# Attention with mixture of experts: the turned sums move to the second pass's ring, and the scaling of the outputs to GpSimd

## The chip, the cores and the metric

The kernel runs on one core of a Trainium2 chip. The metric is the device time of one execution in microseconds (us), as the median of several runs. The engines are TensorE (PE, with its weight loads as PEld), VectorE (DVE), ScalarE (ACT), GpSimd (POOL) and SyncE (SP), which only issues DMAs here. SBUF is the working memory, PSUM the memory that TensorE writes and that VectorE and ScalarE read.

## The reference

The input `x` has shape (8, 1024, 256). With `xn` the layer norm of `x`, the result is

```
x + attention(xn) + ffn(xn)
kqv   = xn @ W_kqv.T                      # 16 heads of 16
score = q @ k / 16 + slope[h] * (n - s)   # per head, key position n, query position s
attention = softmax(score) @ v
ffn = sum over the two best of 8 experts of w * swiglu_e(xn), plus a shared swiglu
```

The softmax needs, for each query of each head, the maximum of its 1024 scores; both sums over keys (of `exp * v` and of `exp`) come from one matrix product, since `v` carries a column of ones.

## The kernel before

Three stages follow each other: `front` (layer norm, projections, shared expert, routing), `experts` (the routed experts, whose results go to a scratch tensor `yr`) and `attend` (attention, and the combination of everything into the output). The change is in `attend` alone.

`attend` works through 32 groups, each of four heads (`GH`) of one batch (8 batches, 4 groups each). A group has 64 units (`UNITS`), in two halves of 32 (`HALF`); a half is 512 queries (`HQ`) against 8 blocks of 128 keys (`NK`) for four heads. In a document like this one a pair is two successive units, and pair k of a group begins with unit 2k.

In each unit `n` TensorE issues one `score` (128 keys by 512 queries, into `p2`, a ring of three PSUM banks) and one half of a maximum unit of the next group (`max_half`, into `p1`, a ring of two tiles, each of two banks). In every odd unit it adds four `products` (probabilities by values, into `p_o`), for a block of keys whose exponentials are done: in units 4k+1 and 4k+3 for units 4k-4 to 4k-1. ScalarE takes the exponential of each `p2` bank into `probs`. VectorE reduces each `p1` tile of 128 by 1024 to its maxima (`max_unit`), one in each pair; eight of them make a chunk, which `join` (two inputs in SBUF) combines to eight columns of `neg`. So one group's first pass (maxima) runs beside the previous group's second pass.

The maxima must become a row of `q_op`. For each of the four chunks of a group `turn_max` transposes `neg` on TensorE into a `p2` bank, ScalarE copies the 8 rows to `m_row`, and SP sends them by two DMAs. The turns are placed by hand: the own group's chunk 3 after unit 5 (`OWN_TURN`), the next group's chunks 0, 1 and 2 after units 21, 37 and 53 (`TURN_AT`).

The output of a half leaves in this way. After unit 3 of the following half ScalarE copies `p_o` to `o_sb` (`output_copy`). After unit 13 (`OUT_TURN`) TensorE transposes it in four pieces into an entry of the first pass's ring `p1` (`turn_output`). VectorE, in its place among the maxima, inverts the sums (`reciprocal`, L1216) and multiplies (L1220) into `att`, a ring of two batches; it adds one to `s1_read` only then, and the ring has two places, so the next maximum unit on TensorE needs the reduction before the output to have ended.

GpSimd waits until four groups of a batch are in `att`, and then, in loops with registers, combines its eight blocks one after another (`combine`): loads of `base` and two gathers from `yr`, the addition of `att`, two scalings and two additions, a store. The last batch is combined by VectorE from terms gathered ahead (`last_terms`, `final`).

Every engine runs its instructions in program order. The groups are written out for all engines but GpSimd.

Of the kernel before, what the change touches and what calls it, by code (L numbers as in the profile page):

```python
# [16 lines left out]
F32 = mybir.dt.float32  # L17
# [5 lines left out]
ds = bass.ds  # L23
# [927 lines left out]
def attend(nc, keep, scratch, out):  # L951
    with ExitStack() as ctx:
# [9 lines left out]
        neg = [sb(f"neg{i}", [P, 8], F32R) for i in range(2)]  # L962
        m_row = [sb(f"m_row{i}", [8, P], F32R) for i in range(4)]
        o_sb = [sb(f"o_sb{i}", [P, HQ]) for i in range(2)]
        rec = sb("rec", [P, 4, GH])
# [6 lines left out]
        col_i = [sb(f"col_i{i}", [P, 2], I32) for i in range(2)]  # L972
        col_w = [sb(f"col_w{i}", [P, 2]) for i in range(2)]
# [11 lines left out]
                 "ex_ok w_ready dve_w pool_c o_st0 o_st1 c_ok base_in0 base_in1 yg_in0 yg_in1 fin_base fin_y "  # L985
# [4 lines left out]
        m_in = [sem(f"t_m_in{c}") for c in range(4)]  # L990
# [9 lines left out]
        OUT_ENTRY = (OUT_TURN + 1) // 2  # L1000
        SIDE = HQ // 2
        R1 = MAX_UNITS + 2
        R2 = UNITS + CHUNKS
        K_LOAD = 14

        def ring1(g, first):
            return MAX_UNITS if first else g * R1 + (MAX_UNITS - 1)

        def bank1(first, r):
            return ((MAX_UNITS if first else MAX_UNITS - 1) + r) % 2  # L1010

        def ring2(g):
            return g * R2 + (CHUNKS - 1)

        def bank2(u, r):
            return (CHUNKS - 1 + (R2 % 3) * u + r) % 3

        def turn_entry(c):
            at = sorted([OWN_TURN, *TURN_AT])
            n = OWN_TURN if c == CHUNKS - 1 else [a for a in TURN_AT if TURN_AT[a] == c][0]  # L1020
            return n + 1 + at.index(n)

        assert R1 % 2 == 0

# [15 lines left out]
        def _(sp):  # L1040
# [26 lines left out]
            def send_max(g, u, chunks, entry):  # L1067
                for c in chunks:
                    half, pair = divmod(c, PAIRS)
                    sp.wait_ge(s["s2_read"], entry(c) + 4)  # L1070
                    for x in range(2):
                        r = 64 * x + S2_ROWS - 1
                        sp.dma_start(q_op[u][r:r + 1, pair, half * HQ:(half + 1) * HQ]
                                     .rearrange("o (q c) -> o q c", q=4).bitcast(F32),
                                     m_row[c][4 * x:4 * x + 4].bitcast(F32)).then_inc(m_in[c], 16)
# [3 lines left out]
            send_max(0, 0, range(CHUNKS - 1), lambda c: c)  # L1079

            def group(g, u, turn, has_prev, has_next):
# [6 lines left out]
                entry = lambda c: ring2(g) + turn_entry(c)  # L1088
                send_max(g, u, [CHUNKS - 1], entry)
                if has_next:  # L1090
                    send_max(g + 1, following(u, turn)[0], range(CHUNKS - 1), entry)
# [15 lines left out]
        def _(pool):  # L1107
# [9 lines left out]
            for i in range(2):  # L1117

                pool.dma_start(scratch["credit"][i], wts[:, 0, 0:1]).then_inc(s[f"o_st{i}"], 16)

            CPB = 7

            def combine(n, u, turn, ring):

                c = Chain(pool, s["pool_c"], n * CPB + 1, s["passed"])
                pool.dma_start(base_c[u][:], scratch["base"][ds(n * P, P)]).then_inc(s[f"base_in{u}"], 16)  # L1126
                c.link(g_.tensor_copy(col_w[u][:], wts[:, :, ds(n, 1)].rearrange("p a o -> p (a o)")))
                c.link(g_.tensor_copy(col_i[u][:], slot_i[:, :, ds(n, 1)].rearrange("p a o -> p (a o)")))  # L1128
                for k in range(2):
                    g_.indirect_dma_start(y_c[k][u][:], None, scratch["yr"],  # L1130
                                          bass.IndirectOffsetOnAxis(col_i[u][:, k:k + 1], 0)).then_inc(s[f"yg_in{u}"], 16)
                hold(pool, s[f"base_in{u}"], 16 * (turn + 1), s["passed"])
                hold(pool, s[f"o_st{u}"], 16 * (turn + 1), s["passed"])
                acc = base_c[u]
                c.link(g_.tensor_tensor(acc[:], acc[:], att[:, ds(ring, 1)].rearrange("p o d -> p (o d)"), ALU.add))
                hold(pool, s[f"yg_in{u}"], 32 * (turn + 1), s["passed"])
                for k in range(2):
                    y = y_c[k][u]
                    c.link(g_.tensor_scalar(y[:], y[:], col_w[u][:, k:k + 1], None, ALU.mult))  # L1139
                    c.link(g_.tensor_tensor(acc[:], acc[:], y[:], ALU.add))  # L1140
                assert c.k == CPB
                pool.sem_inc(s["c_ok"], 1)
                pool.dma_start(out[ds(n * P, P)], acc[:]).then_inc(s[f"o_st{u}"], 16)
# [3 lines left out]
            for q in range(NK):  # L1147
                hold(pool, s["s1_read"], R1 + CHUNK * (q + 1), s["passed"])
# [5 lines left out]
            GB = H // GH  # L1154
            with pool.Fori(0, B - 1) as b:

                hold(pool, s["s1_read"], b * (GB * R1) + (ring1(GB, False) + OUT_ENTRY + 3), s["passed"])
                with pool.Fori(0, NK // 2) as i:
                    for u in range(2):
                        combine(b * NK + i * 2 + u, u, b * (NK // 2) + i, (b % 2) * NK + i * 2 + u)  # L1160
# [307 lines left out]
```

## Time and profile before

| What | us |
|---|---|
| median of 3 runs | 2621.71 (2620.36 to 2624.32) |
| profiled execution, its own time | 2615.34 |
| its span, first to last instruction | 2613.7 |
| first unit of the second pass begins | 1230.55 |
| last `final` on VectorE begins | 2609.16 |

| Engine | busy us | share of the span |
|---|---|---|
| PE | 2438.0 | 93% |
| DVE | 1949.5 | 75% |
| ACT | 1545.0 | 59% |
| POOL | 790.3 | 30% |

The shares are over the three stages. Those of the attention are read from its own stretch: in a stretch, a line gives the busy time of each engine and the number of its instructions in brackets. In the timeline each line is a start, a length, an engine, a source line and the operation with its output and input; several like instructions stand in one line with their count, and in square brackets stands how long the engine was idle before and who ended that.

### The profile page before, as it was taken

The page shows a single profiled execution, that of the slowest core. Times are in us where ns is not written, and L with a number is a line of the kernel's source. Part 1 is how long each engine was busy: PE and PEld are TensorE (multiplying, and loading weights), DVE is VectorE, ACT ScalarE, POOL GpSimd, SP SyncE. Part 2 cuts the span into 40 slices and gives each one's busy share as a digit, 9 for nine tenths or more (in the row PEclk, how much of TensorE's full clock was granted, in tenths as well). Part 3 has the DMA queues.
Part 4 walks back from the last instruction along what each step waited for, and adds up shares of the span by engine and source line. Part 5 has one row for each costly group of instructions (what it writes and reads, how often), then busy time and mean ns, then how long its engine had stood idle before and what let it go on. Part 6 is the DMA issues. An engine that isn't in the chain of part 4 may idle for free.

```text
span 2613.7 us, 56931 instructions
## 1 busy us (share of the span) xinstructions
PE 2438.0 (93%) x19376; PEld 1487.8 (57%) x19377; DVE 1949.5 (75%) x2945; ACT 1545.0 (59%) x3215; POOL 790.3 (30%) x1004
## 2 busy tenths in 40 slices
PE   7999999963999999964999999999999999999998
PEld 5888888862999999861333333333333333333333
DVE  5666666643555555537899999999999999999994
ACT  3333333332333333320788888888888888888887
POOL 2222222235222222250101523505425135052250
PEclk9999999986999999985999999999999999999999
DMA  6999888740222222216324343534434353435330
GB/s 182 177 174 179 154 146 145 129 66 21 70 69 70 69 68 68 67 45 99 71 46 73 78 81 66 98 50 91 81 61 93 59 89 77 73 73 87 56 72 23
DMA packets 178264, 228.51 MB, mean 87 GB/s; under 512 B 43069, under 2 KB 127805, under 8 KB 178057
## 3 DMA queue, kind: packets, MB, share of 16 engines
q1 hardware_dynamic: 153336, 172.15, 36.7%
q0 software_dynamic: 22560, 50.69, 7.8%
q8 instruction: 131, 2.15, 0.4%
q10 hardware_dynamic: 2176, 3.02, 0.3%
q14 instruction: 61, 0.49, 0.1%
HBM read 131.60 MB, written 93.79 MB: 86 GB/s over the span
## 4 chain that ended last, share of the span: by engine, by line
PE 40%; DVE 13%; issue 1%; SPq 0%; DMA 0%; POOLq 0%; POOL 0%; ACT 0%; DVEq 0%
PE p_o L1358 17%; PE p L1348 15%; DVE part L1200 13%; PE p L1335 7%; PE p L1341 1%; DMA k_op<-ali_scratch 0%; POOLq L1113 0%; POOL q_op L1112 0%; SPq L1059 0%; ACT probs L1309 0%; SPq L1046 0%; PE p L1368 0%; ACT o_sb L1296 0%; DVE fin L1182 0%; DVE fin L1183 0%
## 5 line engine op out<-in xcount | busy, mean ns | idle before, releaser
L1200 DVE TENSOR_REDUCE part<-p 128x2 f32<-128x1024 f32 x1024 | 1248.8, 1225 | 95.8 <-PE p L1335 88.3
L1309 ACT ACTIVATE probs<-p 128x512 f32<-128x512 f32 x2048 | 1113.1, 597 | 232.0 <-PE p L1348 199.5
L1335 PE MATMUL p<-k_op,q_op 50*128 50x512 f32 x2048 | 759.5, 462 | 46.9 <-DMA k_op<-ali_scratch 36.6
L1348 PE MATMUL p<-q_op,k_op 51*128 51x512 f32 x2048 | 758.5, 451 | 25.9 <-DVE part L1200 25.9
L1358 PE MATMUL p_o<-probs,v_op 128*32 128x256 f32 x8192 | 656.2, 392 | 4.9 <-ACT o_sb L1296 0.8
L1348 PEld LDWEIGHTS p<-q_op,k_op 51*128 51x128 f32 x2048 | 316.4, 185 | 448.7 <-ACT probs L1309 369.5
L1358 PEld LDWEIGHTS p_o<-probs,v_op 128*32 128x32 f32 x8192 | 163.2, 108 | 338.1 <-ACT probs L1309 258.8
L1335 PEld LDWEIGHTS p<-k_op,q_op 50*128 50x128 f32 x2048 | 307.5, 189 | 61.9 <-issue 36.8
L763 POOL DMA_INDIRECT xe<-xn_scratch,ids x136 | 129.0, 948 | 393.0 <-DMA ids<-lists_scratch 386.4
L857 ACT CAST ht_hi<-pe_h 128x256 fp32r<-128x256 f32 x136 | 50.7, 373 | 289.8 <-PE pe_h L793 289.8
L1126 POOL DMA_DIRECT2D base_c<-base_scratch x56 | 32.2, 575 | 476.0 <-DVE att L1220 463.7
L320 POOL DMA_INDIRECT lists_scratch<-token,slot_c x128 | 127.0, 992 | 79.0 <-DVE slot_c L432 40.2
L564 PE MATMUL p_u<-xt_hi,s_gu_hi 128*128 128x512 f32 x352 | 141.4, 402 | 3.1 <-DVE s_dn_lo L452 3.1
L517 ACT CAST h_hi<-h_sb 128x512 fp32r<-128x512 f32 x96 | 59.5, 620 | 139.0 <-DVE h_sb L385 135.8
L564 PE MATMUL p_u<-xt_hi,s_gu_lo 128*128 128x512 f32 x352 | 138.3, 393 | 0.0
L564 PE MATMUL p_u<-xt_lo,s_gu_hi 128*128 128x512 f32 x352 | 138.1, 392 | 0.0
L867 DVE TENSOR_TENSOR xet_lo<-pe_x,xet_hi 128x256 fp32r<-128x256 f32 x136 | 57.8, 425 | 105.5 <-ACT xet_hi L843 104.9
L1130 POOL DMA_INDIRECT y_c<-yr_scratch,col_i x112 | 112.9, 1008 | 66.3 <-POOL col_i L1128 44.5
L1139 POOL TENSOR_SCALAR y_c<-y_c,col_w 128x256 f32<-128x256 f32 x112 | 103.9, 927 | 87.0 <-DMA y_c<-yr_scratch,col_i 72.8
L309 POOL TENSOR_TENSOR root<-ve,half 128x4 f32<-128x4 f32 x16 | 21.9, 1366 | 333.3 <-DVE ve L339 333.3
L895 DVE TENSOR_TENSOR ht_lo<-pe_h,ht_hi 128x256 fp32r<-128x256 f32 x136 | 57.8, 425 | 86.5 <-ACT ht_hi L858 86.5
L803 PE MATMUL pe_y<-wdn_hi,ht_hi 128*128 (+1 forms) x408 | 118.8, 291 | 3.2 <-DVE ht_lo L896 1.4
(177 smaller groups left out, 4137.2 us busy)
## 6 DMA issues: line engine op xcount, KB each, us to landing
qk_scratch<-qk_out SPq DMA_DIRECT2D x64, 512.0 KB
k_op<-qk_scratch SPq DMA_DIRECT2D x192, 128.0 KB
q_op<-qk_scratch SPq DMA_DIRECT2D x192, 128.0 KB
yr_scratch<-y SPq DMA_DIRECT2D x136, 128.0 KB, 1.7
v_scratch<-v_out SPq DMA_DIRECT2D x16, 1024.0 KB, 13.8
v_op<-v_scratch SPq DMA_DIRECT2D x32, 512.0 KB, 9.5
x<-in_x SPq DMA_DIRECT2D x16, 512.0 KB, 4.7
xn_scratch<-xn SPq DMA_DIRECT2D x16, 512.0 KB
```

Source lines behind the costliest of these rows:

```text
L320: g.indirect_dma_start(scratch["lists"], bass.IndirectOffsetOnAxis(slot_c[n % 2][:, k, b:b + 1], 0), token[:, n * TB + b:n * TB + b + 1], ...
L517: a.copy(h_hi[j % HR][rows], h_sb[j % 2][rows]).then_inc(s["h_hi_ok"], 1)
L564: last = t.matmul(dst, lhs[a](k), rhs[b](k), start=(n == 0), stop=(n == 3 * KD - 1))
L763: g.indirect_dma_start(x_sb[u][:], None, scratch["xn"], bass.IndirectOffsetOnAxis(ids[u][:], 0)).then_inc(rt[f"x_in{u}"], 16)
L803: last = t.matmul(p_y[:, 0:D], ht[a][par][0:rows, c], dn[b][0:rows, ds(off + c * D, D)], start=(i == 0 and sub == 0), stop=(i == all_ - 1 ...
L1130: g_.indirect_dma_start(y_c[k][u][:], None, scratch["yr"], bass.IndirectOffsetOnAxis(col_i[u][:, k:k + 1], 0)).then_inc(s[f"yg_in{u}"], 16)
L1139: c.link(g_.tensor_scalar(y[:], y[:], col_w[u][:, k:k + 1], None, ALU.mult))
L1200: v.tensor_reduce(part[c_ % 2][:, kh, :, qb], p1[bank][:], AX.X, ALU.max, negate=True).then_inc(s["s1_read"], 1)
L1309: a.activation(probs[kb % 4][:, h], p2[bank2(u, r)][:], ACT.Exp).then_inc(s["s2_read"], 1)
L1335: return t.matmul(p1[bank][:, x], q_op[u][lo:lo + S1_ROWS, pair, q0:q0 + P], k_op[u][lo:lo + S1_ROWS, pair, kh * 512:(kh + 1) * 512], star ...
L1348: t.matmul(p2[bank][:], k_op[u][lo:lo + S2_ROWS, pair, kb * P:(kb + 1) * P], q_op[u][lo:lo + S2_ROWS, pair, half * HQ:(half + 1) * HQ], st ...
L1358: ins = t.matmul(p_o[32 * h:32 * h + 32, cols], v_op[u][:, kb, VW * h:VW * h + VW], probs[kb % 4][:, h, cols], start=(kb == 0 and side == ...
```

## The change

- The transposed sums take an entry of the second pass's ring `p2` instead of the first pass's ring `p1`. ScalarE copies 17 columns of each 32 (16 sums with values and the sum of exponentials) to a new SBUF tile `o_t`, waits for its own copy, and tells VectorE by `o_out`.
- VectorE only inverts the sums, from `o_t`, after maximum unit 11 of the half. GpSimd multiplies into `att` (`normalise`). Only the very last half keeps the old way (`output_last`).
- The four transposes of maxima per group become two of 16 columns: after unit 5 for the own group's second half, after unit 37 for the next group's first half. Before the first group there is one instead of three. SP sends four DMAs after each.
- GpSimd's program is written out: each half has one `normalise`, then one block combined (of the batch before), then the loads of the next block. Its loops, its small copies by register, and the waits on the credits go. The last batch's gathers come one block per half in the first eight halves.
- In the last group VectorE does `last_terms` after both inversions, at the end, and not between the halves.

```diff
-        TURN_AT = {2 * CHUNK * c + 21: c for c in range(CHUNKS - 1)}
+        TURN_AT = HALF + 5
         OWN_TURN = 5
-        OUT_COPY, OUT_TURN = 3, 13
+        OUT_COPY, OUT_TURN, OUT_SEEN = 3, 13, 11
-        R1 = MAX_UNITS + 2
-        R2 = UNITS + CHUNKS
+        R1 = MAX_UNITS
...
+            def normalise(x_no):
+                g, half = divmod(x_no, 2)
+                b, hg = divmod(g, H // GH)
+                pool.wait_ge(s["rec_ok"], x_no + 1)
+                o = o_t[x_no % 2]
+                dst = att[:, (b % 2) * NK + 4 * half:(b % 2) * NK + 4 * half + 4, hg * (GH * HD):(hg + 1) * (GH * HD)]
+                g_.tensor_tensor(dst.rearrange("p q (h c) -> p q h c", h=GH), o[:, :, :, 0:HD],
+                                 rec[x_no % 2][:, :, :, None].to_broadcast([P, 4, GH, HD]), ALU.mult).then_inc(s["att_ok"], 1)
...
+            for x_no in range(2 * GROUPS - 1):
+                normalise(x_no)
+                if x_no < NK:
+                    last_batch(x_no)
+                else:
+                    pool.wait_ge(s["att_ok"], x_no + 1)
+                    combine(x_no - NK)
+                if x_no >= NK - 1:
+                    fetch(x_no - NK + 1)
+            combine(first - 1)
...
-            def output(g, half, use, bank):
-                dve.wait_ge(s["s1_ps"], use + 1)
-                ot = p1[bank][:, 0].rearrange("p (q h c) -> p q h c", q=4, h=GH)
-                v.reciprocal(rec[:], ot[:, :, :, HD]).then_inc(s["rec_ok"], 1)
-                dve.wait_ge(s["c_ok"], b * NK + NK)
-                dve.wait_ge(s["rec_ok"], x_no + 1)
-                v.tensor_tensor(dst.rearrange("p q (h c) -> p q h c", h=GH), ot[:, :, :, 0:HD],
-                                rec[:, :, :, None].to_broadcast([P, 4, GH, HD]), ALU.mult).then_inc(s["s1_read"], 1)
+            def invert(x_no):
+                dve.wait_ge(s["o_out"], x_no + 1)
+                if x_no >= 2:
+                    dve.wait_ge(s["att_ok"], x_no - 1)
+                v.reciprocal(rec[x_no % 2][:], o_t[x_no % 2][:, :, :, HD]).then_inc(s["rec_ok"], 1)
...
+            def turned_copy(g, half, use):
+                x_no = 2 * g + half
+                act.wait_ge(s["s2_ps"], use + 1)
+                if x_no >= 2:
+                    act.wait_ge(s["att_ok"], x_no - 1)
+                ot = p2[use % 3][:].rearrange("p (q h c) -> p q h c", q=4, h=GH)
+                a.copy(o_t[x_no % 2][:], ot[:, :, :, 0:HD + 1]).then_inc(s["s2_read"], 1)
+                act.wait_ge(s["s2_read"], use + 4)
+                act.sem_inc(s["o_out"], 1)
...
-            def turn_output(g, half, use, bank):
+            def turn_output(g, half, use):
                 pe.wait_ge(s["o_ok"], g * 2 + (half + 2))
-                pe.wait_ge(s["s1_read"], use + 1)
+                pe.wait_ge(s["s2_read"], use + 1)
                 for q in range(4):
-                    ins = t.transpose(p1[bank][:, 0, q * P:(q + 1) * P], o_sb[half][:, q * P:(q + 1) * P], ident[:])
-                ins.then_inc(s["s1_ps"], 1)
+                    ins = t.transpose(p2[use % 3][:, q * P:(q + 1) * P], o_sb[half][:, q * P:(q + 1) * P], ident[:])
+                ins.then_inc(s["s2_ps"], 1)
```

## Rows read from the trace of the kernel before

**Rows 1.** Stretches: busy us of each engine (instructions), granted clock, DMA share, GB/s.
```profile
1700.00:1742.70 42.70, 42.02 (x398) 16.16 (x397) 40.41 (x41) 35.93 (x71) 3.01 (x4) 1.00 0.35 55
```

**Rows 2.** Waits from 1300 to 2500 us: us in total, times, longest.
```profile
PE p L1348 <- DVE part L1200: 16.2, 57, 0.3
```

**Rows 3.** Timeline of PE, start of a half with the turn after unit 5.
```profile
1714.43 0.50 PE L1348 MATMUL p<-q_op,k_op 51*128 51x512 f32 x1
...
1716.01 0.50 PE L1348 MATMUL p<-q_op,k_op 51*128 51x512 f32 x1
...
1717.34 0.50 PE L1348 MATMUL p<-q_op,k_op 51*128 51x512 f32 x1
```

**Rows 4.** The same half, the turned output after unit 13.
```profile
1721.05 0.66 PE L1368 MATMUL p<-ident,o_sb 128*128 128x128 f32 x4
1721.99 0.47 PE L1348 MATMUL p<-q_op,k_op 51*128 51x512 f32 x1 [0.28 <-DVE part L1200]
...
1723.23 0.50 PE L1348 MATMUL p<-q_op,k_op 51*128 51x512 f32 x1
```

**Rows 5.** The same half, the pair of the turn after unit 21.
```profile
1725.71 0.50 PE L1348 MATMUL p<-q_op,k_op 51*128 51x512 f32 x1
...
1727.15 0.50 PE L1348 MATMUL p<-q_op,k_op 51*128 51x512 f32 x1
```

**Rows 6.** Timeline of the last group, where no maxima are left: its turned output.
```profile
2594.62 0.66 PE L1368 MATMUL p<-ident,o_sb 128*128 128x128 f32 x4
...
2595.20 0.51 PE L1348 MATMUL p<-q_op,k_op 51*128 51x512 f32 x2
2595.38 0.26 DVE L1216 RECIPROCAL rec<-p 128x16 f32<-128x16 f32 x1 [11.91 <-PE p L1368]
```

**Rows 7.** Timeline of DVE: reductions that wait for nobody, and the inversion.
```profile
1194.64 5.75 DVE L1200 TENSOR_REDUCE part<-p 128x2 f32<-128x1024 f32 x5 [28.70 <-PE p L1335]
...
1721.76 0.25 DVE L1216 RECIPROCAL rec<-p 128x16 f32<-128x16 f32 x1
1722.11 0.42 DVE L1220 TENSOR_TENSOR att<-p,rec 128x256 f32<-128x256 f32 x1
```

**Rows 8.** ScalarE by source line (ns: least/median/most) and in the timeline.
```profile
L1296 ACT COPY o_sb<-p_o x64: 586/592/593, 1265.9 to 2607.0; 128x512 f32<-128x512 f32 x64
...
L1292 ACT CAST m_row<-p x128: 238/239/255, 1206.3 to 2571.1; 8x128 fp32r<-8x128 f32 x128
...
1723.76 1.09 ACT L1309 ACTIVATE probs<-p 128x512 f32<-128x512 f32 x2 [0.18 <-PE p L1348]
```

**Rows 9.** All joins (ns: least/median/most); one that met GpSimd: POOL, DVE, PE.
```profile
L1207 DVE TENSOR_TENSOR neg<-part x128: 154/157/719, 1203.8 to 2568.0; 128x8 fp32r<-128x8 f32 x128
...
2012.04 0.75 POOL L1135 TENSOR_TENSOR base_c<-base_c,att 128x256 f32<-128x256 f32 x1
...
2012.11 0.72 DVE L1207 TENSOR_TENSOR neg<-part 128x8 fp32r<-128x8 f32 x1
...
2014.11 0.47 PE L1348 MATMUL p<-q_op,k_op 51*128 51x512 f32 x1 [0.28 <-DVE part L1200]
```

**Rows 10.** Timeline of POOL: one block combined, the next one's loads; landing of gathers.
```profile
2522.60 0.75 POOL L1135 TENSOR_TENSOR base_c<-base_c,att 128x256 f32<-128x256 f32 x1
...
2526.60 0.92 POOL L1139 TENSOR_SCALAR y_c<-y_c,col_w 128x256 f32<-128x256 f32 x1 [0.21 <-POOL base_c L1140]
...
2529.21 0.63 POOL L1143 DMA_DIRECT2D out<-base_c  x1 [0.78 <-POOL base_c L1140]
...
2532.29 1.04 POOL L1130 DMA_INDIRECT y_c<-yr_scratch,col_i  x1 [0.82 <-POOL col_i L1128]
...
DMA to landing us min/median/max: 2.7/2.8/9.7
```

**Rows 11.** The end: DVE in the timeline; landing of the final stores.
```profile
2609.16 1.23 DVE L1240 TENSOR_TENSOR att<-att,fin 128x1024 f32<-128x1024 f32 x1
...
DMA to landing us min/median/max: 2.9/3.3/3.7
```

More of the change, by code:

```diff
@@ L1065, in load, with send_max @@
                              .rearrange("(k p) c -> p k c", p=P)).then_inc(v_in[u], 16)
[L1067 to L1070, printed above, removed]
+            def send_max(g, u, half, use):
+                sp.wait_ge(s["s2_read"], use + 4)
+                for pair in range(PAIRS):
                     for x in range(2):
@@ L1116, in _, with last_batch @@
             pool.wait_ge(s["w_ready"], 1)
[L1117 to L1143, printed above, removed]
+            c = Chain(pool, s["pool_c"], 1)
             first = (B - 1) * NK
             pool.dma_start(fin[:, 0], scratch["base"][first * P:].rearrange("(q p) d -> p q d", p=P)).then_inc(s["fin_base"], 16)
-            for q in range(NK):
-                hold(pool, s["s1_read"], R1 + CHUNK * (q + 1), s["passed"])
+            def last_batch(q):
                 for k in range(2):
@@ L1248, in group @@
             def group(g, u, turn, has_prev, has_next):
[L1249 removed]
                 due = None
[L1251 to L1254 removed]
+                for w in range(MAX_UNITS):
+                    if has_next:
+                        max_unit(ring1(g) + w, w)
                         if due is not None:
@@ L1258, in group @@
                         if w % CHUNK == CHUNK - 1:
-                            due = (w // CHUNK, base + (r + 2))
-                        w += 1
-                    if n % HALF == OUT_TURN and (n >= HALF or has_prev):
-                        pg, ph = (g, 0) if n >= HALF else (g - 1, 1)
-                        output(pg, ph, base + r, bank1(not has_prev, r))
-                        r += 1
-                        if not has_next and n >= HALF:
-                            half0 = base + (r + 2)
-                    if n == HALF - 1 and not has_next:
-                        last_terms()
+                            due = (w // CHUNK, ring1(g) + (w + 3))
+                    for half in range(2):
+                        if w == half * (MAX_UNITS // 2) + OUT_SEEN and (half or has_prev):
+                            invert(2 * g + half - 1)
                 if due is not None:
@@ L1271, in group @@
                 if not has_next:
-                    final(0, half0)
-                    output(g, 1, base + r, bank1(not has_prev, r))
-                    final(1, base + (r + 3))
+                    last_terms()
+                    dve.wait_ge(s["att_ok"], 2 * GROUPS - 1)
+                    final(0)
+                    output_last(g, 1, use2(g, UNITS))
+                    dve.wait_ge(s["rec_ok"], 2 * GROUPS + 1)
+                    final(1)
             groups(dve, group)
```

187 lines of the change are left out of this document (91 added, 96 removed).

## The prediction

> **What bounds the kernel now.** I first read the page's chain that ended last: its attention part consists of TensorE and VectorE lines in turn, so the two are nearly level and a share of busy time can't decide. Then the stretch of one middle group [rows 1]: 42.70 us, in which PE is busy 42.02 and DVE 40.41, at a granted clock of 1.00, the level of 2.4 GHz. The waits say which of them is late: TensorE stood still for VectorE's maxima only 16.2 us in 28 groups, 57 times, so twice a group and always for the same thing [rows 2]. Last the timeline, for the distance from the first score of a pair to that of the next. A plain pair takes 1.24 us (1723.23 - 1721.99 [rows 4]); 1.238 is the mean of the plain pairs. ScalarE's two exponentials of a pair fill 1.09 us [rows 8] and VectorE's reduction can follow its forerunner after (5.75 - 1.23) / 4 = 1.13 us [rows 7]. So **TensorE's own issue sets the pace**, with 0.1 us per pair left on VectorE. Everything above 32 x 1.238 = 39.62 us in a group of 42.75 is what TensorE does or waits for besides, and it stands at the same places in every half of 21.38 us:
>
> - pair 2, turn after unit 5 or 37: 1716.01 - 1714.43 = 1.58, so 0.34 over [rows 3]; and pair 3 after it: 1.33, 0.09 over [rows 3]. The turn itself is 0.2 of that, by the next item; the rest comes from ScalarE, which copies `p_o` at this place.
> - pair 10, turn after unit 21 or 53: 1727.15 - 1725.71 = 1.44, 0.20 to 0.21 over [rows 5].
> - turned output after unit 13: from its first transpose to the next score 1721.99 - 1721.05 = 0.94 [rows 4].
>
> The sum is 0.34 + 0.09 + 0.21 + 0.94 = 1.58 per half, and 16 x 1.238 + 1.58 = 21.39: nothing is missing.
>
> **The change, part by part.**
>
> *Two turns of maxima fewer per group.* Those after units 21 and 53 go, those after 5 and 37 stay, each now with 16 columns for 8. The transpose streams the same 128 columns, so I leave its 0.20 as it is; pairs 2 and 3 keep their 0.43. Gain: 2 x 0.207 = 0.41 us per group. Where the rows are needed: chunk 1's join comes after maximum unit 16 (unit 33), before the turn at 37 as now. SP sends four DMAs together instead of two and two: both halves are wanted about 27 units (17 us) later, so that hides. SP's queue order stays the same, and its loads for the group after next come first as now. Before the first group, two turns go that lie in VectorE-bound time: nothing.
>
> *The turned output leaves the ring of the maxima.* Now the next maximum unit needs the reduction ahead of the output to have ended (the inversion behind it begins at 1721.76 [rows 7], and TensorE, which was idle for it, goes on at 1721.99 [rows 4]). In the new ring the bank was read two units before, and the two places of `p1` belong to maxima alone, where the reduction of two pairs before has ended 0.4 us before it is needed. What stays is the transposes' own cost. The last group shows it, since no maxima run there: 2595.20 - 2594.62 = 0.58 [rows 6]. Gain: 0.94 - 0.586 = 0.353 per half.
>
> *ScalarE gets the turned copy.* No row has it. Its neighbours are 239 ns for 128 columns and 592 for 512 [rows 8]; on the line between them 272 columns cost 0.37 us. The bounds are 0.24 and, since it is read in short pieces, 0.8 us. Then it waits for its own end and sends a semaphore; VectorE's inversion and its multiplication, which waits for it, begin 0.35 apart with 0.25 of work [rows 7], so 0.10. Who is behind it: VectorE can start on the turned tile 0.18 us after the next score on TensorE (2595.38 - 2595.20 [rows 6]), so ScalarE is free again at 0.15 + 0.37 + 0.10 = 0.62 to 0.7 us after that score, where its next exponential would have begun at 0.53 [rows 3, 4 and 8]. It is 0.1 to 0.17 late. The two exponentials behind it are due for the products of unit 17, which begin 0.66 us into their pair, that is 1.24 + 0.66 = 1.90 after the score; the second exponential would end at 1.63 and now ends at 1.77. So **it fits with about 0.1 to spare**, and costs nothing; if the copy takes 0.5 or more, each further tenth is a tenth per half. The copies of the dropped turns give ScalarE 0.24 back elsewhere.
>
> *VectorE* loses the multiplication (0.42) and keeps an inversion of 0.25 [rows 7] after maximum unit 11, five pairs behind the copy, so it never waits for `o_out`. It takes 0.2 to 0.3 of a slack of 0.4 and regains 0.1 per pair. It doesn't become the bound: 16 x 1.13 + 0.25 + 2 x 0.1 = 18.5 us per half against the new 20.8.
>
> *GpSimd.* Per half now: normalise (0.75 taken from the like addition, bounds 0.7 and 1.5 for its pieces), a combine of three additions, two scalings and four gaps, 3 x 0.75 + 2 x 0.92 + 4 x 0.2 = 4.9, the store with 0.78 + 0.63, the loads with 0.63 (as the store's issue) + 0.82 + 2 x 1.04 + 0.3 (a gap between the two gathers, estimated) [rows 10]: 11 us of 20.8. The loads have most of a half to land (2.8, at worst 9.7 us [rows 10]). Whoever waits for GpSimd (ScalarE's copy and the inversion, both for the normalise of two halves before) waits for something long done.
>
> *A join against a GpSimd operation.* Where a join began 0.07 us behind a GpSimd addition, it took 0.72 instead of 0.16 us, and two pairs later TensorE stood idle for 0.28 behind VectorE, in a place where it has no such wait else [rows 9]. The Trainium skill, SBUF — State Buffer, "Who interferes with whom", says that a VectorE operation with two SBUF inputs and a GpSimd one that reads SBUF exclude each other for the whole instruction. This row agrees, and the join's median of 0.157 beside a longest of 0.719 [rows 9] says that it is rare in this trace, though GpSimd is busy for 30% of the span. By my times the new order puts VectorE's inversion at 0.8 to 1.05 us into pair 12, GpSimd's arithmetic at 1.2 to 7.0, and the joins at 7.0 (first half) and 5.75 (second half, inside a scaling begun 0.6 before). I count nothing for it, and keep it as a rival.
>
> *The end.* The last group has no turn at 37 and no maxima; its two turned copies delay ScalarE by 0.1 each, a loss of 0.2. But GpSimd's last work now hangs behind it. In the times of before: transposes at 2594.62, VectorE can look at 2595.38 [rows 6], copy and own wait to 2595.8, inversion to 2596.2, normalise to 2597.1, combine of block 54 to 2602.1, its store to 2603.5, loads of block 55 with the second gather issued at 2606.3 and landed 2.8 later at 2609.1, combine to 2614.0, store issued at 2614.8, landed at about 2617. The old end is 2609.16 + 1.23 + 3.3 = 2613.7 [rows 11]. So **the span ends on GpSimd**, 3.3 us later than VectorE's path (bounds 2 and 6). `last_terms` moves into time in which VectorE is idle for more than 10 us [rows 6], so nothing.
>
> **Sum.** Groups 1 to 30: 30 x 2 x (0.207 + 0.353) = 33.6 us. Group 0: 2 x 0.207 + 0.353 = 0.8. Last group: -0.2. End: -3.3. Together 30.9 us less: the profiled span 2613.7 becomes 2582.8. The median of the runs is 6.4 us above the time of the profiled execution (2621.71 to 2615.34); I take the same difference off it: **2591 us**, 1.2% less. A group goes from 42.75 to 41.63 us.
>
> **Rivals.**
>
> *A, the turned copy is late.* For it: the margin is only 0.1 us and the copy's cost is no row. With 0.6 us for the copy, 0.2 per half, 62 halves: 12 us back, 2603; with a small excess 2597. Against: a copy of 512 columns, with twice the work, costs 0.59.
>
> *B, joins meet GpSimd.* One join per half, or one per group, held for up to 0.56 us, of which TensorE sees 0.15 to 0.28 [rows 9]: 31 x 0.16 to 62 x 0.16 = 5 to 10 us back, 2596 to 2601. It decides when a GpSimd addition begins within 0.2 us ahead of a join [rows 9], which a normalise slower by 0.5 us would bring about in each half alike. The exclusion of the whole instruction on the skill's page, SBUF — State Buffer, is the rule behind this rival.
>
> *C, no tail.* If GpSimd is quicker in the last group, or the store isn't the last thing: 2587.5.
>
> *D, slower.* GpSimd paces the halves: ScalarE's copy waits for `att_ok` of two halves before, and behind that copy stand the exponentials. It decides from a GpSimd round of 20.8 us; mine is 11, so the normalise with its broadcast operand would have to take over 10 us instead of 0.74. With a round of 22 us, 62 x (22 - 21.38) = 38 us are added: 2660. Nothing in the rows is near that.
>
> *E, it doesn't do what it says.* TensorE still waits at the output, now for ScalarE's copy, and only the two turns bring something: 30 x 0.41 + 0.4 - 3.3 = 9.4, so 2612.
>
> **How the numbers follow.** Forecast 0.60 (own range 2587 to 2595), A 0.15, B 0.11, C 0.07, D 0.03, E 0.04. The range leaves out D and E and the upper end of A and B together: 2584 to 2605. A measurement of this kernel tells about 0.2% (5 us) from no change. Everything but D is faster by more: 0.95; the same 0.02; slower 0.03.
>
> **What would show it.** Plain pairs still 1.24 us. The step over the turned output 0.58 to 0.6 with no idle behind VectorE's reductions; pair 10 at 1.24; pairs 2 and 3 unchanged. A copy of 0.37 to 0.4 us on ScalarE, and the product after unit 17 not waiting for an exponential. A normalise below 1 us, GpSimd idle half the time, joins at 0.16 us, and a POOL store as the last thing, 3 us behind VectorE's. A plain pair above 1.24, a join of 0.7 in each half, or idle time of TensorE behind ScalarE in pair 8 would make the prediction wrong.

## The result and the profile after

The changed kernel takes 2586.31 us (median of 4 runs, 2584.93 to 2588.60) against 2621.8 us (median of 4 runs, 2620.36 to 2624.32): a ratio of 0.9853 with a 95% interval of 0.983 to 0.9876. That ratio, like those below, is not the quotient of the two medians, which is 0.9865 and lies in the interval. On another chip, with the experiments below, the same two kernels gave 2583.76 and 2615.22 us, a ratio of 0.9885 (0.9861 to 0.9909). The forecast was 2591 us, 30.9 us less; the medians differ by 35.5 us at first and by 31.5 us the second time. The profiled execution has a span of 2583.1 us, where the sum gave 2582.8.

Two lines of the page of the changed kernel: its span, and busy time with share of the span and instructions.

```profile
span 2583.1 us, 55232 instructions
...
PE 2420.8 (94%) x19312; PEld 1480.6 (57%) x19313; DVE 1913.7 (74%) x2882; ACT 1556.7 (60%) x3214; POOL 806.1 (31%) x953
```

One middle group of the changed kernel, which answers to [rows 1]; it is 41.67 us long.

```profile
1695.92:1737.59 41.67, 41.58 (x400) 15.84 (x396) 39.42 (x39) 36.45 (x71) 15.80 (x21) 1.00 0.41 78
```

All that TensorE's matmuls waited for from 1300 to 2500 us in the changed kernel. This answers to [rows 2]: the 57 waits for VectorE's maxima, 16.2 us, are gone.

```profile
PE p L1355 <- ACT probs L1317: 0.6, 1, 0.6
```

PE in the timeline of that group: the pair with the turn (1699.66), a plain pair (1703.77 to 1705.01), the turned output with the score behind it, the pairs after it. This answers to [rows 3, 4].

```profile
1699.66 0.48 PE L1355 MATMUL p<-q_op,k_op 51*128 51x512 f32 x1
...
1701.21 0.50 PE L1355 MATMUL p<-q_op,k_op 51*128 51x512 f32 x1
...
1702.53 0.50 PE L1355 MATMUL p<-q_op,k_op 51*128 51x512 f32 x1
...
1703.77 0.50 PE L1355 MATMUL p<-q_op,k_op 51*128 51x512 f32 x1
...
1705.01 0.50 PE L1355 MATMUL p<-q_op,k_op 51*128 51x512 f32 x1
...
1706.25 0.66 PE L1375 MATMUL p<-ident,o_sb 128*128 128x128 f32 x4
1706.84 0.50 PE L1355 MATMUL p<-q_op,k_op 51*128 51x512 f32 x1
...
1708.08 0.49 PE L1355 MATMUL p<-q_op,k_op 51*128 51x512 f32 x1
...
1709.31 0.50 PE L1355 MATMUL p<-q_op,k_op 51*128 51x512 f32 x1
```

What the reader is to see: from the transposes to the next score 1706.84 - 1706.25 = 0.59 us, where it was 0.94, and no idle time before that score; plain pairs at 1.24 as before; pair 2 at 1701.21 - 1699.66 = 1.55 and pair 3 at 1.32, for 1.58 and 1.33 before (the 0.02 that pair 2 is shorter stands in pair 1); pair 8 (1708.08 to 1709.31) at 1.23, so nobody waits for the delayed exponentials.

The tile `o_t` of the changed kernel by source line (ns, least/median/most), and ScalarE around one copy in the timeline.

```profile
L1299 ACT COPY o_t<-p x63: 385/385/387, 1268.8 to 2560.0; 128x272 f32<-128x272 f32 x63
L1213 DVE RECIPROCAL rec<-o_t x63: 243/244/254, 1275.6 to 2560.4; 128x16 f32<-128x16 f32 x63
L1124 POOL TENSOR_TENSOR att<-o_t,rec x63: 613/617/721, 1275.9 to 2560.8; 128x256 f32<-128x256 f32 x63
```

```profile
1706.94 0.39 ACT L1299 COPY o_t<-p 128x272 f32<-128x272 f32 x1 [0.31 <-PE p L1375]
1707.44 1.76 ACT L1317 ACTIVATE probs<-p 128x512 f32<-128x512 f32 x3
```

The copy is 0.385 us (0.37 was interpolated), and the exponential begins 1707.44 - 1706.84 = 0.60 us after the score (0.62 to 0.7 was worked out). GpSimd's multiplication takes 0.617 us, less than the 0.75 taken.

The end of the changed kernel, POOL in the timeline from the last normalise on, and VectorE's last addition; this answers to [rows 10, 11].

```profile
2560.76 0.72 POOL L1124 TENSOR_TENSOR att<-o_t,rec 128x256 f32<-128x256 f32 x1 [9.96 <-DVE rec L1213]
...
2566.43 0.64 POOL L1148 DMA_DIRECT2D out<-base_c  x1 [0.30 <-POOL base_c L1147]
...
2569.43 0.56 POOL L1132 DMA_DIRECT2D base_c<-base_scratch  x1 [2.36 <-issue]
...
2573.78 1.23 DVE L1243 TENSOR_TENSOR att<-att,fin 128x1024 f32<-128x1024 f32 x1
...
2574.92 0.72 POOL L1143 TENSOR_TENSOR base_c<-base_c,att 128x256 f32<-128x256 f32 x1 [2.28 <-DMA y_c<-yr_scratch,yslot_i]
...
2579.58 0.64 POOL L1148 DMA_DIRECT2D out<-base_c  x1 [0.30 <-POOL base_c L1147]
```

GpSimd's last store begins 4.6 us after VectorE's last addition has ended, so the span ends on GpSimd.

To see where the time went, the attention is cut at the first score of groups 0, 1 and 31, and at the end of the span. These are sums of whole stretches, from the starts of the scores in each trace (us):

| kernel (execution) | second pass begins | group 0 | groups 1 to 30 | group 31 and end | span |
|---|---|---|---|---|---|
| before | 1230.6 | 53.9 | 1282.7 | 46.6 | 2613.7 |
| changed | 1228.4 | 51.5 | 1251.6 | 51.7 | 2583.1 |
| before, again | 1233.9 | 61.5 | 1283.4 | 46.6 | 2625.3 |
| changed, again | 1229.4 | 50.3 | 1250.4 | 51.6 | 2581.8 |

The columns of groups 1 to 30 and of group 31 repeat to about 1 us in each kernel; those of the start and of group 0, where the forecast gave the change 0.8 us, don't.

### The profile page after: what moved, and what is told of

It is laid out like the page before. It is cut to its first block, busy times and chain, and to the rows that moved or that the text cites. A ratio compares the mean times of both kernels' runs of the same rounds, so it can differ in the third digit from the quotient of the medians.

```text
span 2583.1 us, 55232 instructions
## 1 busy us (share of the span) xinstructions
PE 2420.8 (94%) x19312; PEld 1480.6 (57%) x19313; DVE 1913.7 (74%) x2882; ACT 1556.7 (60%) x3214; POOL 806.1 (31%) x953
## 4 chain that ended last, share of the span: by engine, by line
issue 27%; POOL 17%; PE 7%; DVE 2%; DMA 0%; SPq 0%; POOLq 0%
POOL y_c L1134 4%; POOL y_c L1146 4%; POOL base_c L1147 3%; PE p_o L1365 3%; PE p L1355 2%; DVE part L1197 2%; POOL base_c L1143 2%; POOL out L1148 1%; POOL att L1124 1%; POOL base_c L1132 1%; PE p L1342 1%; DMA k_op<-ali_scratch 0%; POOLq L1102 0%; POOL q_op L1101 0%; SPq L1050 0%
## 5 line engine op out<-in xcount | busy, mean ns | idle before, releaser
L1124 POOL TENSOR_TENSOR att<-o_t,rec 128x256 f32<-128x256 f32 x63 | 39.0, 619 | 793.6 <-DVE rec L1213 793.6
L1134 POOL DMA_INDIRECT y_c<-yr_scratch,yslot_i x112 | 112.5, 1005 | 36.3 <-issue 36.3
L876 DVE COPY y<-pe_y 128x256 f32<-128x256 f32 x136 | 57.7, 425 | 79.3 <-PE pe_y L803 79.3
```

The costliest lines, as they stand in the source:

```text
L1134: g_.indirect_dma_start(y_c[k][u][:], None, scratch["yr"], bass.IndirectOffsetOnAxis(slot_i[:, k, n:n + 1], 0)).then_inc(s[f"yg_in{u}"], 16)
```

## The experiments

All ratios are to the kernel before on the same chip, with a 95% interval. "Group" is the median time of groups 1 to 30 unless it says mean. The runs were made in three rounds on three chips, and the median of the kernel before was 2630.95 us (two turns alone, VectorE scales too, blocks stored before the end), 2628.22 us (plain loads, output's way alone, two copies, busy GpSimd) and 2615.22 us (changed kernel again, weights first, both). So times of different rounds can't be compared.

**Two turns alone.** The kernel before with `neg` and `m_row` of 16 columns and rows, and with:

```diff
-        TURN_AT = {2 * CHUNK * c + 21: c for c in range(CHUNKS - 1)}
+        TURN_AT = HALF + 5
-        R2 = UNITS + CHUNKS
+        R2 = UNITS + 2
```

> The kernel before with only the two turns of maxima per group; the output keeps the first pass's ring and VectorE's scaling. My theory (TensorE's own issue sets the pace, the dropped turns and the output's ring add up): pair 10 and pair 26 fall from 1.44 to 1.24 us, the step over the turned output stays 0.94 us, a group takes 42.75 - 0.41 = 42.34 us, the whole 12.5 us less than before (about 2609), so a bit over a third of the change's gain. Rival (the turns were hidden, the gain is the ring's): groups stay at 42.75 and the time at 2622. Rival (fewer turns also free ScalarE and VectorE): more than 0.5 us per group.

Measured: 0.9969 (0.9949 to 0.999), 2619.61 us: 3 to 13 us less than the kernel before beside it, where 12.5 was expected. Pairs 10 and 26 fell to 1.24 us, but the mean group of this profile is 42.86 us, no less than before: in 20 groups TensorE was late by 0.2 us or more, up to 1.07 us in one pair, mostly in pair 22. PE and POOL in its timeline at such a place:

```profile
1527.84 0.50 PE L1344 MATMUL p<-q_op,k_op 51*128 51x512 f32 x1
1528.37 0.50 PE L1344 MATMUL p<-q_op,k_op 51*128 51x512 f32 x1
1529.84 0.63 PE L1364 MATMUL p<-ident,o_sb 128*128 128x128 f32 x4
1530.97 0.47 PE L1344 MATMUL p<-q_op,k_op 51*128 51x512 f32 x1 [0.50 <-DVE part L1196]
```

```profile
1526.57 0.97 POOL L1126 DMA_INDIRECT y_c<-yr_scratch,col_i  x1 [0.30 <-issue]
1527.57 0.74 POOL L1131 TENSOR_TENSOR base_c<-base_c,att 128x256 f32<-128x256 f32 x1
```

The second score of the pair comes 0.53 us after the first instead of 0.34, the products behind it are late too, and then VectorE is late for the output: 1.13 us from transposes to score instead of 0.94. Nothing in the profile releases that second score. Two further runs were made for this.

**The same with plain loads for gathers.**

```diff
-                    g_.indirect_dma_start(y_c[k][u][:], None, scratch["yr"],
-                                          bass.IndirectOffsetOnAxis(col_i[u][:, k:k + 1], 0)).then_inc(s[f"yg_in{u}"], 16)
+                    pool.dma_start(y_c[k][u][:], scratch["yr"][ds(n * P, P)]).then_inc(s[f"yg_in{u}"], 16)
```

> The kernel before with two turns alone, but the two gathers of each block that GpSimd combines are plain loads of as many rows, issued from the same place (so the output's routed part is another row's; the last batch's gathers stay). In the turns-alone kernel all stalls of TensorE over 0.15 us (33 of them in 30 groups, most at pairs 22 and 0) began 0.4 to 4 us behind the issue of a gather. Theory A (a gather's transfers make TensorE's issue late): the stalls at pairs 0, 1, 12 and 22 go, groups at 42.35 to 42.4, about 14 us less than the turns-alone kernel in its profile. Theory B (any GpSimd transfer, or where the program's pieces lie, does it): stalls stay, the mean group is 42.6 to 42.9.

Measured: 0.9923 (0.9898 to 0.9948), group 42.38 us, mean 42.44. The groups are as theory A had them. The profiled execution is only 8 us shorter than that of the turns alone and not 14, since its second pass began later (1233.6 for 1231.9 us) and its group 0 took 56.2 us for 53.7. But:

**Two turns alone, a second execution.**

> The kernel before with two turns alone, for a second profile. If the stalls of TensorE behind GpSimd's gathers belong to this program's moments, the same groups (5, 6, 9, 10, 12 to 14 and so on) are long again, above all at pair 22, and the mean group is 42.8 to 42.9. If they were an accident of that one execution, the mean is 42.4 as with plain loads.

Measured (one run, 2605.57 us beside 2612.87): mean group 42.30 us, and pair 22 at 2.17 us; only three pairs of 30 groups are late by over 0.15 us. So the stalls were an accident of the first execution, and the plain loads can't be credited with their absence. The mean over the groups is 0.45 us below that of before (42.76), as expected for two dropped turns (0.41).

**The output's way alone.** The changed kernel with four turns of eight columns:

```diff
-        TURN_AT = HALF + 5
+        TURN_AT = {2 * CHUNK * c + 21: c for c in range(CHUNKS - 1)}
...
-                    if l == 0:
-                        pe.wait_ge(m_in[half], (g + 1) * (32 * PAIRS))
+                    if l == 0 or l == PAIRS:
+                        pe.wait_ge(m_in[half * PAIRS + l // PAIRS], g * 32 + 32)
```

> The changed kernel with the four turns of maxima of before (units 5, 21, 37, 53, eight columns each), so the output's way alone is changed. My theory (the terms add up): pairs 10 and 26 are 1.44 us again, the step over the turned output stays 0.59, a group takes 41.67 + 0.41 = 42.08 us, the whole 12.7 us more than the changed kernel. Rival (what the turns alone showed: in a kernel with other moments for GpSimd's gathers, stalls of TensorE eat the gain, so turns are worth nothing here either): groups at 41.67 to 41.8.

Measured: 0.9904 (0.9868 to 0.9939), group 42.07 us, where 42.08 was expected. Pairs 10 and 26 are 1.44 us again, and the output's step is 1724.01 - 1723.43 = 0.58. PE in its timeline:

```profile
1723.43 0.66 PE L1378 MATMUL p<-ident,o_sb 128*128 128x128 f32 x4
1724.01 0.50 PE L1358 MATMUL p<-q_op,k_op 51*128 51x512 f32 x1
```

With this and the runs before it the two parts are measured apart and add up. As mean groups: 42.76 without either, 42.30 with the turns alone (second execution), 42.11 with the output alone, 41.68 with both (second execution). The turns give 0.46 and 0.43, the output's way 0.65 and 0.62.

**VectorE scales too.** The changed kernel, with the multiplication behind the inversion on VectorE:

```diff
-                g_.tensor_tensor(dst.rearrange("p q (h c) -> p q h c", h=GH), o[:, :, :, 0:HD],
-                                 rec[x_no % 2][:, :, :, None].to_broadcast([P, 4, GH, HD]), ALU.mult).then_inc(s["att_ok"], 1)
...
                 v.reciprocal(rec[x_no % 2][:], o_t[x_no % 2][:, :, :, HD]).then_inc(s["rec_ok"], 1)
+                dve.wait_ge(s["rec_ok"], x_no + 1)
+                v.tensor_tensor(dst.rearrange("p q (h c) -> p q h c", h=GH), o_t[x_no % 2][:, :, :, 0:HD],
+                                rec[x_no % 2][:, :, :, None].to_broadcast([P, 4, GH, HD]), ALU.mult).then_inc(s["att_ok"], 1)
```

> The changed kernel, but VectorE multiplies too, from the copied sums in SBUF, right behind its inversion; GpSimd only combines. My theory (GpSimd's scaling is off the path and VectorE has slack): groups stay at 41.67 us within 0.05, because 0.42 + 0.25 + gaps = 0.75 us per half stands against 2.2 us of VectorE's slack per half; at most 0.1 to 0.3 us is seen at pair 12 or 13, since the slack at one place is only 0.4 us. So 0 to +6 us over the changed kernel (2586 to 2592), and the end on GpSimd is up to 0.7 us earlier. Rival (taking the multiplication from VectorE was what freed TensorE): groups go back towards 42.4 and the time to about 2608.

Measured: 0.9914 (0.9881 to 0.9948), group 42.39 us: 0.72 more than the changed kernel. Pair 13 is 1.53 us in each half (0.29 over), pair 4 1.33 (0.09 over). DVE and, in the second fence, PE in its timeline:

```profile
1704.92 0.24 DVE L1203 RECIPROCAL rec<-o_t 128x16 f32<-128x16 f32 x1
1705.27 0.43 DVE L1210 TENSOR_TENSOR att<-o_t,rec 128x256 f32<-128x256 f32 x1
1705.62 3.48 DVE L1187 TENSOR_REDUCE part<-p 128x2 f32<-128x1024 f32 x3
```

```profile
1705.45 0.50 PE L1353 MATMUL p<-q_op,k_op 51*128 51x512 f32 x1
...
1706.98 0.47 PE L1353 MATMUL p<-q_op,k_op 51*128 51x512 f32 x1 [0.22 <-DVE part L1187]
```

VectorE's next reduction begins 1705.62 - 1704.92 = 0.70 us behind the inversion's start. That is more than the 0.4 us which a reduction may be late here, so TensorE waits, in each half again. The expectation had this pair right and its sum wrong: 0.3 us in 62 halves is 18 us, not 6. Of the 0.70 us, 0.29 reach TensorE, which gives the 0.4 once more. The rival was right: it said 42.4 us for the group, and about 2608 us for the whole, where 2608.78 us was measured (in a round in which the kernel before, too, was 9 us above its first median). That GpSimd scales is worth 0.7 us of a group. Without it a group gains 42.77 - 42.39 = 0.38 us over the kernel before, no more than the two turns alone give, so the output's new ring gains next to nothing by itself.

**Two copies on ScalarE.**

```diff
+                a.copy(o_u[:], ot[:, :, :, 0:HD + 1])
                 a.copy(o_t[x_no % 2][:], ot[:, :, :, 0:HD + 1]).then_inc(s["s2_read"], 1)
```

> The changed kernel, but ScalarE copies the turned sums twice, first into a tile that nobody reads, then as before. The first copy puts 0.29 to 0.39 us more on ScalarE ahead of two exponentials that my sum had 0.1 to 0.17 us to spare for (the products of unit 17 wait for them). My theory (the slack at that place counts): pair 8 and pair 24 grow by 0.1 to 0.3 us, a group by 0.2 to 0.6 us, from 41.67 to 41.9 to 42.3; the whole 6 to 18 us over the changed kernel. Rival (ScalarE's idle time over the whole half, 3 us, counts): groups stay at 41.67.

Measured: 0.9869 (0.9839 to 0.9898), group 41.93 us, with 1.37 for 1.24 us in pairs 8 and 24 alone. The extra copy has 0.386 us and puts ScalarE back by about 0.29, and 0.13 of it reaches TensorE: the slack at this place is about 0.15 us, as worked out, not the (41.67 - 36.45) / 2 = 2.6 us that ScalarE idles in a half.

**A busy GpSimd.** Eight additions more in every half of the changed kernel:

```diff
+                for _ in range(8):
+                    c.link(g_.tensor_tensor(junk[:], junk[:], junk2[:], ALU.add))
                 if x_no >= NK - 1:
                     fetch(x_no - NK + 1)
```

> The changed kernel, but GpSimd makes eight additions more in every half, each of 256 columns on tiles of its own, right behind the block that it combines; each starts 0.93 us behind the one before, so that one of two joins of a group, or both, falls on a GpSimd operation. Rival B of the prediction (a join that meets GpSimd is held up to 0.56 us, of which TensorE sees 0.15 to 0.28): joins of 0.3 to 0.7 us appear in many halves, a group grows by 0.1 to 0.4 us, 3 to 12 us in all. Rival D (GpSimd paces the halves): not yet, its round is 11 + 7.5 = 18.5 us of 20.8; if my sum of its round is too low by 2.3 us, the groups grow to twice its round. If neither is true: groups at 41.67 and the end 7.5 us later, because the additions stand ahead of the last block too.

Measured: 0.9895 (0.9864 to 0.9925). The last part is 62.1 us for 51.7, 10.4 us more and not 7.5: GpSimd came 2 us late to the last but one block, since it was still at work on the one before, and its last eight additions took 8.2 us. Its joins by source line (ns), and in the second fence one long join and the GpSimd addition that it met:

```profile
L1210 DVE TENSOR_TENSOR neg<-part x128: 156/158/971, 1201.7 to 2536.1; 128x8 fp32r<-128x8 f32 x128
```

```profile
1867.10 0.73 POOL L1150 TENSOR_TENSOR base_c<-base_c,y_c 128x256 f32<-128x256 f32 x1
...
1867.23 0.62 DVE L1210 TENSOR_TENSOR neg<-part 128x8 fp32r<-128x8 f32 x1
```

Which operation a join met, and when, decides what it costs. Of its 128 joins 45 began inside a GpSimd addition of two inputs (0.73 us long). 42 of them ended 0.75 to 0.76 us after that addition's start, so with it, wherever they had begun; the other three began in its last 0.1 us and kept their 0.157. Of 13 that began inside a scaling (0.92 us) three were held, all to 0.49 us after its start, and ten that began 0.39 us in or later were not. Of 20 that began inside a DMA issue of GpSimd 19 kept their 0.16 us; the last is the longest, 0.971 us: an addition began 0.17 us behind it, and it ended with that addition. In all, 47 joins took over 0.2 us and 15 of them 0.46 us or more. The group is 41.77 us, 0.1 more. So rival B is real and small: with GpSimd at work for most of the half it costs 3 us in all. In the changed kernel itself 27 joins, one in nearly every group in which GpSimd combines, fall 0.37 us into an addition and take 0.39 us, the longest 0.405; TensorE's pairs 1 and 2 together are no longer for it. The Trainium skill, SBUF — State Buffer, "Who interferes with whom", has the later of the two blocked for the whole of the other. The additions agree with it; the scalings don't, since they held a join for the first 0.49 of their 0.92 us alone.

**Blocks stored before the end.** The changed kernel, with two blocks combined instead of one in halves 57 and 58:

```diff
+            def blocks_at(x_no):
+                n = x_no - NK
+                if n < 0 or x_no == 2 * GROUPS - 2:
+                    return []
+                if x_no < first + 1:
+                    return [n]
+                return [m for m in ((n, n + 1) if x_no == first + 1 else (n + 1, n + 2) if x_no == first + 2 else (n + 2,)) if m < first]
```

> The changed kernel, but GpSimd combines two blocks instead of one in two of the halves of the last batch, so that all blocks are stored before the last group's outputs. My theory (the last 5 us are GpSimd's chain: combine, loads, gather, combine, store): the span ends on VectorE's last addition and its store, about 5 us earlier than the changed kernel's (span 2578 for 2583, time about 2581), groups unchanged but for at most 0.5 us where two blocks stand in one half. Rival (the end is set by the stores' landing or by VectorE): under 1 us.

Measured: 0.9834 (0.9802 to 0.9867), 2588.27 us; the part from group 31 on is 47.0 us instead of 51.7, groups unchanged at 41.69. The expected span of 2578 us didn't come (2592.4): this execution's second pass began at 1237.7 us, and its group 0 took 56.0. POOL in its timeline: the last operation is the last normalise, and VectorE's last addition comes 13 us later.

```profile
2574.78 0.72 POOL L1124 TENSOR_TENSOR att<-o_t,rec 128x256 f32<-128x256 f32 x1 [13.14 <-DVE rec L1223]
```

```profile
2587.84 1.22 DVE L1253 TENSOR_TENSOR att<-att,fin 128x1024 f32<-128x1024 f32 x1
```

**The changed kernel again.**

> The changed kernel itself again, as the measure for the two that follow. Over the profiles so far the start of the second pass lay between 1228.4 and 1237.7 us and group 0 took 51.5 to 62.0 us with the same instructions, while the median of the other groups repeated to 0.02 us. If these two places make the spread of the runs, groups 1 to 30 are at 41.67 us again and the difference to the first profile of the changed kernel stands in the start and in group 0 alone. Ratio 0.984 to 0.988.

Measured: 0.9885 (0.9861 to 0.9909), 2583.76 us; group 41.67. The ratio is a little above the 0.984 to 0.988 expected. **And the kernel before again:**

> The kernel before once more, for a second profile. If the median of the runs of before lies above the profiled execution because of the start and of group 0 (clock at 1.2 GHz for longer), then groups 1 to 30 take 42.75 us on average again and the last part 46.6, and the whole difference to the first profile stands in the start (1230.6 there) and in group 0 (53.93 there). If groups or the end differ by more than 1 us in all, this reading is wrong.

Measured (one run): 2626.93 us, 14 us over the other run of the same kernel beside it, 2612.87. Its groups 1 to 30 differ from the first profile by 0.7 us and its end not at all, but group 0 takes 61.5 us for 53.9 and begins 3.3 us later. The granted clock (before the DMA share) shows why. First the first maxima in the kernel before, then one stretch of group 0 in the changed kernel, and last the same stretch and two later ones in the kernel before again:

```profile
1195.00:1228.00 33.00, 23.17 (x60) 8.29 (x59) 32.90 (x32) 0.77 (x3) 0.00 (x0) 0.50 0.41 63
```

```profile
1246.00:1253.00 7.00, 7.00 (x72) 2.65 (x72) 6.78 (x7) 6.24 (x12) 0.00 (x0) 1.00 0.01 2
```

```profile
1246.00:1253.00 7.00, 7.00 (x44) 2.10 (x36) 3.89 (x4) 3.33 (x7) 0.00 (x0) 0.50 0.46 58
1253.00:1260.00 7.00, 7.00 (x42) 2.60 (x40) 4.12 (x5) 3.25 (x6) 1.15 (x2) 0.50 0.35 95
1260.00:1267.00 7.00, 7.00 (x41) 2.19 (x37) 3.68 (x3) 3.38 (x7) 0.87 (x1) 0.50 0.13 38
```

TensorE is busy all of the time in both stretches of group 0, but at 1.2 GHz (0.50) it issues 41 to 44 matmuls in 7 us, where it issues 72 at 2.4 GHz (1.00). It was at 1.2 GHz already in the first maxima, in which it is busy for 23.17 of 33 us, after it had stood for 36.57 us until the first keys were loaded (kernel before, up to 1193.81 us). Then it stands for 8 us of pair 1 while VectorE works out the routing weights. How many of the next pairs (2.16 us each instead of 1.24) pass before the clock rises differs from execution to execution, from two in the changed kernel again to more than ten here.

**Weights first,** in the changed kernel:

```diff
+            weights()
             for w in range(MAX_UNITS):
                 max_unit(w, w)
                 if w % CHUNK == CHUNK - 1:
                     join(w // CHUNK, w + 3)
-            weights()
```

> The changed kernel, with VectorE's fourteen operations for the routing weights before the first maxima, where it waits 28.7 us for the operands of the first group, and not behind them, where TensorE waits 9 us for it. My theory (the 9.06 us of pair 1 of group 0 are lost on the path): pair 1 falls from 9.06 to at most 2.5 us; the clock of TensorE, at 1.2 GHz there, can then rise sooner or later than now. Group 0 at 43 to 50 us for 51.5 or more, the whole 5 to 11 us less than the changed kernel. Rival (the first maxima are delayed by the weights as much as is saved): no change.

Measured: 0.9858 (0.9837 to 0.9879), 2578.09 us, 5.7 less than the changed kernel on the same chip. In its profile pair 1 is 1.53 us for 9.06 and group 0 44.7 for 50.3. VectorE has the weights ready at 1174.4 us and then waits another 20.2 us, so the first maxima aren't delayed by them (first one at 1193.7 us, in the kernel before at 1193.8). The next pairs still take 2.48 and 2.16 us until the clock rises: the slow pairs are not the doing of the stall in pair 1. **And both:**

> Both: weights first, and all of GpSimd's blocks stored before the last outputs. The two gains lie at the two ends and add up: 4.7 us (the tail, measured) and what the weights alone give; the whole 10 to 16 us less than the changed kernel, about 2573, ratio 0.979 to 0.982.

Measured: 0.9841 (0.9817 to 0.9865), 2574.69 us (2570.57 to 2578.34), 9.1 us less than the changed kernel's 2583.76 beside it. This is the fastest of the versions in its round; the end is 46.6 us as expected, and group 0 took 48.4 us in its profile, since the clock rose later than with the weights alone (44.7). The gain lies just below the 10 to 16 us expected, and the ratio above 0.979 to 0.982.

## Why the prediction came out as it did

- **What bounds the kernel.** Right. TensorE's issue paced it before and does now: plain pairs kept their 1.24 us in every run, TensorE's 16.2 us of waits for VectorE are gone, and each removed piece of TensorE's time or wait came out of the groups (but for the first execution of the turns alone, with its stalls).
- **The two turns.** 0.41 us per group was forecast; 42.07 - 41.67 = 0.40 was measured. That the turn behind `output_copy` keeps its 0.43 held as well.
- **The output's step.** 0.353 per half was forecast, from the last group, where no maxima run; pair 6 fell from 2.169 to 1.827, by 0.342, and in the second pair of profiles from 2.185 to 1.817, by 0.368. Taking this price from a stretch where the rival for the wait is missing was the best step of the working.
- **ScalarE's copy.** 0.37 interpolated, 0.385 measured; fits, with about 0.15 us to spare (two copies). Rival A is refuted for this kernel, and it was close: 0.29 us more on ScalarE does cost.
- **VectorE's part.** Right that it doesn't become the bound. But the prediction gave GpSimd's scaling no price of its own: it said that the output leaves the ring, and that VectorE loses 0.42. The run with VectorE's multiplication shows that without that part the group would gain 0.38 instead of 1.10 us. The price of an edit that other edits protect has to be asked for each alone.
- **GpSimd.** Its round, from a normalise to the last gather's issue, is 9.2 us (median) for the 11 forecast, so rival D is out. Normalise takes 0.617 for 0.75. The joins were not all at 0.16 us as forecast: 27 of 128 met an addition and took 0.39, which cost TensorE nothing. So rival B's meeting came, once in a group, and its price didn't.
- **The end.** The mechanism was right and its size was off: 3.5 us were forecast (3.3 and the 0.2 of the last group), and it is 51.66 - 46.58 = 5.1, in the second pair of profiles 5.0. The term missed is 2.36 us of idle time between the store of one block and the load of the next (2569.43), which no wait explains. The run with early stores took 4.7 us back.
- **The sum for groups 1 to 30.** 33.6 us forecast; 31.0 in the first pair of profiles and 33.0 in the second. In the first the changed kernel has an extra 0.94 us in group 18 and 0.2 in each of groups 1 to 4.
- **The step that failed is the last one, from the profile to the median.** The span came to 2583.1 for 2582.8, though with errors that cancel: 2.6 us too much in the groups and 1.6 too little at the end, against 2.2 us of an earlier start and 2.5 in group 0, of which 0.8 were forecast. Such a hit is luck in part. Then I took the 6.4 us that the median of before lay above its profiled execution as a constant. It was no property of the kernel: in the second profile of before group 0 is 7.6 us longer and begins 3.3 us later, and for the changed kernel the medians lay 1.4 and 0.2 us above the profiled execution. With 1.4 for 6.4 the forecast would have been 2586; so the median, 2586.31 us, came out 4.7 us below 2591: inside the range, outside the forecast's own 2587 to 2595. By the measured ratio (0.9853 of 2621.7 us is 2583.2) it lies just below the range's 2584 as well.

By parts that repeat (groups 1 to 30, the end, the 0.8 forecast in group 0) the change gives 27 to 29 us. The profiles differ beyond that in the start and in group 0 alone; the rest of the medians' 35.5 and 31.5 us must stand there too if their runs are like the profiled ones, which isn't shown. The median of the kernel before itself differs by 16 us between the rounds on three chips, and what part of this a chip has isn't known. Whether the change has a part in the start, by leaving out two turns before group 0 and two small stores, isn't settled: group 0 took 53.9, 61.5 and 62.0 us in the three profiles with four turns and 50.3 to 61.0 us in the nine with two turns and the weights in their old place, so the ranges overlap.

## What to carry to other kernels

Where two engines are nearly level, find the one that never waits in the plain stretch, write down each place that takes longer than the plain step, and price an edit by those places: they added up here to 0.02 us of a 42.75 us group. An engine's idle time over a half is no slack: what counts is how late one instruction may be at its place (0.4 us for VectorE, 0.15 us for ScalarE), and excess is paid once per round. And price the last round by itself, with every engine that has work behind it.

## What the runs showed of the hardware that was not expected

- TensorE's clock, at 1.2 GHz since the first maxima (1195 to 1228 us), stayed there for a time that differed between executions of the same program, though TensorE was busy for 7.00 of 7 us in three stretches one after another: group 0 took 53.9 and 61.5 us in the kernel before. This, with the start of the pass at 1227 to 1238 us, is most of the difference between profiles; everything behind it repeats within some tenths of a us per group, but for the stalls of the next point.
- TensorE can be late by 0.2 to 1.1 us inside a pair with nothing in the profile that it waits for: in one execution in 20 of 30 groups, in the next of the same program in hardly any. Nearly all of these places lay close behind a gather of GpSimd, but so do many undisturbed ones. The cause stays open.
- A join of eight columns, 0.16 us alone, that began inside a GpSimd addition (0.73 us) ended with it, in 42 of 45 cases of the busy GpSimd. Beside a scaling (0.92 us) it was held up to 0.49 us after the scaling's start, beside a DMA issue not at all but once. It took 0.97 us at worst.
- GpSimd stood for 2.36 us ahead of the load of the last block, without a wait that the profile shows. That is no accident: in all nine profiles in which its program is written out it stands there for 2.36 to 2.88 us, and ahead of the first gather of block 28 for 2.48 to 2.71, and ahead of no other load or gather of the blocks for over 1 us. The cause stays open.
